# Four transformer layers on one core: three of six attentions made with the keys on partitions

## The chip, the cores and the metric

One core of one Trainium2 chip runs the kernel. The metric is the device time in microseconds (us) of one execution; less is better. The median of three runs of the kernel before is 3726.12 us (3721.3 to 3736.9).

## The reference

A batch of 64 elements of 128 tokens and 128 features (fp32), with a context of 77 tokens per element, goes through four layers:

- **L0**: self attention (16 heads, rope, causal), cross attention with the context (16 heads, rope, no mask), a gelu MLP of 512.
- **L1**: self attention (16 heads, no mask), cross attention (16 heads, no mask), then a mixture of experts: of 8 experts the two best per token.
- **L2**: a Mamba-2 block, then cross attention with 8 heads and one mask of keys.
- **L3**: cross attention with 16 heads and a mask of pairs, a last layer norm.

```python
s = jnp.einsum('blhd,bmhd->bhlm', q, k)        # 8 features per head; rope on q and k in L0
p = jax.nn.softmax(s, axis=-1)
a = jnp.einsum('bhlm,bmhd->blhd', p, v)
x = x + (a @ wo + bo)
```

## The kernel before

**Tiling.** The batch is cut into 16 passes of four elements (`NB` = 4), and the passes go round four streams, each with tiles of its own; four passes are a group. A pass is a first half (L0, L1 up to the routing) and a second half (the gathered experts' rows, L2, L3). A stream's order is first(g+1), second(g), and so on, so the last second half runs by itself. A fifth stream holds the experts: 20 pairs of blocks per group (`take` and `take_down` fetch rows and weights on the SP queue, then `block_turn`, `block_up`, `block_down`, `give`).

**The six attentions** are the list `ATT`: L0s and L0c in layer 0, L1s and L1c in layer 1, L2c, L3c. L0s and L1s have 128 keys, the others 77; all but L2c have 16 heads. Their steps, per element b:

- `spread` (GpSimd, line 2576): the element's keys times a 0/1 pattern, four heads beside each other, so that one product over 32 rows gives the scores of four heads.
- `scores` (TensorE, lines 1918 and 1923): where there is a mask, a bf16 product that writes it, then four fp32 products on 32 rows each (two on 64 rows for L2c), each into a bank of PSUM of its own. Queries stand on partitions, 4 x 77 or 4 x 128 scores in a bank.
- `soft` (VectorE, lines 2320 and 2326, then ScalarE, line 2155), by halves of eight heads: the maximum over the keys, the subtraction into SBUF, the exponential in place.
- `turn` (TensorE, line 1933, then ScalarE, line 2164), by quads of four heads: each head's probabilities are transposed, because the product with the values needs the keys on partitions, and copied out of PSUM.
- `mix` (TensorE, line 1945, ScalarE, line 2173), by halves: per head one product with the values, which carry a column of ones for the sum; four heads side by side in four column groups.
- `regroup` (TensorE, line 1953, VectorE, lines 2335 and 2336): four transposes back (two for L2c), and the division by the sum.

Ahead of them are norms (lines 2276 to 2279, 2544 to 2547, 2114, 1874, 2135), projections (line 1892; `rope` also multiplies by weights with swapped halves, line 1894, and combines both on VectorE, lines 2296 to 2299) and `values` (lines 1901 and 2307).

**What sets the order.** `timetable` simulates all five streams with a cost for each step (`parts`), the steps it waits for (`inputs_of`) and the free PSUM banks, and takes per engine the step with the least key: its time plus terms from tables (`LEAD`, `PHASES`, `STAY`, `EAGER`, `AHEAD`), which `CHANGES` replaces each 60 us of its plan. `STAY` is the price of a change of ScalarE's function table:

```python
key = (t + lead * (work[n][m] + PHASES[n]) - eager.get((step[0], engine), 0.0) - ahead.get(attention_of(step), 0.0)
       + (stay if switch else 0.0))
```

`Plan` sorts each engine's steps by the result. On the chip each engine runs that fixed list in order and waits on semaphores. The eight banks of PSUM are dealt out by the same plan: four to `scores`, two to `rope`, one to any other step with a product.

## Time and profile before

| | |
|---|---|
| median of three runs | 3726.12 us (3721.3 to 3736.9) |
| profiled execution | 3734.74 us, of which the span of instructions is 3732.9 us |
| mean granted TensorE clock | 0.952 |
| busy: TensorE / its weight loads | 3195.7 us (86%) / 2269.6 us (61%) |
| busy: VectorE / ScalarE / GpSimd | 2605.4 (70%) / 2652.3 (71%) / 1246.9 us (33%) |
| DMA | 212.98 MB, mean 57 GB/s |

PE is the matrix engine, PEld its weight loads (they overlap PE), DVE is VectorE, ACT ScalarE, POOL GpSimd, SP the queue that issues most DMAs. "L1933" is line 1933 of the kernel. A group's row gives what it writes and reads, shapes and count, then busy time and the mean of one; after the bar stand the idle time of the engine just ahead of the group and what ended it. Busy time is a union over the group, so overlapping matmuls are counted once, and busy divided by count is what one costs the engine. An fp32 matmul that isn't a transpose appears as two records.

### The profile page before, as it was taken

What the parts mean: (1) busy time and instruction counts of PE and PEld (TensorE: products, weight loads), DVE (VectorE), ACT (ScalarE), POOL (GpSimd) and SP (SyncE); (2) the same over time, 40 slices, a digit from 0 to 9 for tenths busy, and PEclk for the clock granted to TensorE, in tenths of its full rate; (3) what the DMA queues carried; (4) which work ended last, traced back from release to release, by engine and by line L of the source; (5) the groups of instructions that cost most, each with busy time, mean ns of one, the idle gap of its engine ahead of it and who ended that gap; (6) DMA issues with size and microseconds to landing.
All of it is one profiled execution on the core that took longest, in us unless ns stands there. A gap on an engine that the chain in (4) does not pass through costs nothing.

```text
span 3732.9 us, 87645 instructions
## 1 busy us (share of the span) xinstructions
PE 3195.7 (86%) x30064; PEld 2269.6 (61%) x30064; DVE 2605.4 (70%) x5408; ACT 2652.3 (71%) x5088; POOL 1246.9 (33%) x1615
## 2 busy tenths in 40 slices
PE   6898888888888979998988888998888997777897
PEld 3566556566756657665665656666565665665565
DVE  7877787755477777556888777665888877326775
ACT  4777777777876757887776766788776776656566
POOL 3122333212153353112244244212235434214632
PEclk9999999999999989999999999999999998989899
DMA  7013200134410033221000014322000004442000
GB/s 280 1 43 135 109 6 15 30 97 108 103 37 3 18 100 89 69 64 43 19 22 14 3 44 109 83 72 57 26 23 20 6 19 108 103 112 59 16 2 13
DMA packets 211920, 212.98 MB, mean 57 GB/s; under 512 B 51808, under 2 KB 155168, under 8 KB 211232
## 3 DMA queue, kind: packets, MB, share of 16 engines
q1 hardware_dynamic: 203296, 190.58, 18.1%
q0 software_dynamic: 8192, 16.79, 1.5%
q8 instruction: 252, 4.13, 0.5%
q14 instruction: 180, 1.47, 0.1%
HBM read 135.98 MB, written 71.30 MB: 56 GB/s over the span
## 4 chain that ended last, share of the span: by engine, by line
PE 39%; DVE 23%; ACT 15%; issue 8%; SPq 7%; DMA 4%; POOL 4%; ACTq 0%; DVEq 0%; POOLq 0%
PE ps L1933 8%; DVE mx L2320 6%; PE ps L1923 5%; PE ps L1945 4%; DVE pr L2326 4%; DMA b_up<-cols 4%; ACT block_hid L2211 3%; ACT pt L2164 3%; PE ps L1892 3%; PE ps L1953 2%; PE ps L2005 2%; PE ps L1918 2%; DVE kx L2326 2%; ACT xh L2114 2%; SPq L1818 1%
## 5 line engine op out<-in xcount | busy, mean ns | idle before, releaser
L2320 DVE TENSOR_REDUCE mx<-ps 128x8 f32<-128x616 f32 (+1 forms) x704 | 671.4, 954 | 334.7 <-PE ps L1923 316.4
L2164 ACT ACTIVATE pt<-ps 77x512 f32<-77x512 f32 (+1 forms) x1408 | 768.9, 593 | 126.1 <-PE ps L1933 123.2
L2576 POOL TENSOR_TENSOR kx<-kT,in_tiles 128x308 f32<-128x308 f32 (+1 forms) x384 | 315.7, 822 | 830.5 <-PE ps L1923 740.0
L1933 PE MATMUL ps<-k_sb,pr 128*77 128x128 f32 (+1 forms) x3776 | 538.9, 284 | 33.9 <-ACT pr L2155 10.3
L1933 PEld LDWEIGHTS ps<-k_sb,pr 128*77 128x77 f32 (+1 forms) x3776 | 421.1, 147 | 142.2 <-issue 73.2
L1945 PE MATMUL ps<-pt,v 77*16 77x128 f32 (+2 forms) x11264 | 444.3, 278 | 29.0 <-ACT pt L2164 11.2
L2326 DVE TENSOR_TENSOR pr<-ps,mx 128x616 f32<-128x616 f32 (+1 forms) x472 | 450.3, 954 | 16.2
L2155 ACT ACTIVATE pr<-pr 128x616 f32<-128x616 f32 (+1 forms) x472 | 392.7, 840 | 75.6 <-DVE pr L2326 74.6
L2173 ACT ACTIVATE og<-ps 128x256 f32<-128x256 f32 x704 | 267.3, 381 | 236.8 <-PE ps L1945 233.6
L1923 PE MATMUL ps<-kx,qT 32*128 32x308 f32 (+2 forms) x2816 | 361.6, 547 | 42.2 <-ACT pt L2164 15.8
L1945 PEld LDWEIGHTS ps<-pt,v 77*16 77x16 f32 (+2 forms) x11264 | 251.8, 97 | 181.1 <-issue 85.1
L2544 POOL TENSOR_SCALAR dt_p<-mv 128x4 f32<-128x4 f32 (+1 forms) x144 | 35.3, 245 | 942.8 <-DVE mv L2279 940.5
L1953 PE MATMUL ps<-k_sb,og 128*128 128x128 f32 x1408 | 232.8, 286 | 54.4 <-ACT og L2173 48.1
L1933 PE MATMUL ps<-k_sb,kx 128*77 128x128 f32 (+1 forms) x1856 | 267.2, 284 | 11.1 <-DVE pr L2326 4.7
L1953 PEld LDWEIGHTS ps<-k_sb,og 128*128 128x128 f32 x1408 | 154.7, 143 | 181.7 <-ACT og L2173 71.1
L2114 ACT ACTIVATE xh<-x,dt_p,rstd 128x128 f32<-128x128 f32 x448 | 184.3, 485 | 87.8 <-POOL dt_p L2547 85.9
L1933 PEld LDWEIGHTS ps<-k_sb,kx 128*77 128x77 f32 (+1 forms) x1856 | 208.2, 148 | 63.0 <-issue 33.7
L2326 DVE TENSOR_TENSOR kx<-ps,mx 128x616 f32<-128x616 f32 (+1 forms) x232 | 221.1, 953 | 8.0
L2155 ACT ACTIVATE kx<-kx 128x616 f32<-128x616 f32 (+1 forms) x232 | 194.3, 839 | 45.1 <-DVE kx L2326 44.3
L2335 DVE RECIPROCAL rc<-ps 128x16 f32<-128x16 f32 (+1 forms) x384 | 95.5, 249 | 184.8 <-PE ps L1953 174.1
L1923 PEld LDWEIGHTS ps<-kx,qT 32*128 32x128 f32 (+1 forms) x2816 | 125.1, 189 | 145.1 <-issue 104.9
L2005 PEld LDWEIGHTS ps<-block_cols,w_up 128*128 128x128 f32 x1280 | 183.0, 224 | 35.7 <-issue 14.9
(209 smaller groups left out, 5733.3 us busy)
## 6 DMA issues: line engine op xcount, KB each, us to landing
w_up<-weights SPq DMA_DIRECT2D x160, 256.0 KB
w_down<-weights SPq DMA_DIRECT2D x160, 256.0 KB
sent<-block_hid SPq DMA_DIRECT2D x42, 512.0 KB, 6.3
made<-block_hid SPq DMA_DIRECT2D x42, 512.0 KB, 6.3
block_rows<-sent SPq DMA_DIRECT2D x160, 64.0 KB
b_down<-expert_b SPq DMA_DIRECT2D x160, 64.0 KB
made<-block_out SPq DMA_DIRECT2D x160, 64.0 KB, 2.2
cT<-ctx_cols SPq DMA_DIRECT2D x32, 154.0 KB, 3.1
```

Of the source, the lines that this page charges most:

```text
L1923: i = mm(o, qT[s][r, b * L:(b + 1) * L], spread_keys[s][r, pl.slot(("spread", a, s, b), 2), 0:4 * keys], start=mask is None, stop=True)
L1933: i = tr(p[0:keys, j * L:(j + 1) * L], probs[s][pl.slot(unit, 3)][:, c:c + keys], ident)
L1945: i = mm(ps[32 * j:32 * j + t.slot, pl.banks[step][0], q * L:(q + 1) * L], heads_of(s, t)[0:keys, n, :], pt[s][0:keys, q, j * L:(j + 1) * ...
L1953: i = tr(p[:, q * L:(q + 1) * L], og[:, s % S, q * L:(q + 1) * L], ident)
L2005: i = mm(p[:, c * L:(c + 1) * L], w_up[:, j, c * 128:(c + 1) * 128], block_cols[:, j * L:(j + 1) * L], start=True, stop=True)
L2114: i = go_act(xh[s][0:m, b, :], src[0:m, b, :], ACT.Identity, scale=rstd[s][0:m, b:b + 1], bias=shift[s][0:m, b:b + 1])
L2155: go_act(v, v, ACT.Exp, scale=t.scale).then_inc(probs_ready.sem, 1)
L2164: go_act(pt[s][0:keys, q % 2, :], p[0:keys, :], ACT.Copy).then_inc(probsT_ready.sem, 1)
L2173: go_act(og[:, s % S, 2 * h * L:2 * (h + 1) * L], p[:, 0:2 * L], ACT.Copy)\
L2320: link(v_.tensor_reduce(m, tile, AX.X, ALU.max, negate=True))
L2326: tell(dve, v_.tensor_tensor(dst, tile, m.rearrange("p (c h) -> p c h", c=2).unsqueeze(3).broadcast_to([128, 2, 4, keys]), ALU.add), score ...
L2576: tell(pool, g_.tensor_tensor(spread_keys[s][:, pl.slot(step, 2), 0:4 * keys].rearrange("p (h k) -> p h k", h=4), kT[s][:, b * keys:(b + 1 ...
```

## The change

L0c, L1s and L1c get the mark `flip`; L0c and L1c (16 heads, 77 keys) are `flat` as well. For a marked attention `soft` and `turn` fall away. In their place:

- `scores` as before; `peak` (VectorE) takes only the negated maximum of each head.
- `split` (GpSimd) cuts it into three bf16 pieces, whose sum it is; `shift` turns the pieces on TensorE with one bf16 product, and VectorE copies them to SBUF as bf16.
- `scores_t` (TensorE) makes the scores again with operands exchanged, so that the keys are on partitions, and adds the maximum by a bf16 product with a 0/1 pattern. In L1s that is four chunks, one per head of a quad, of 128 keys; in the flat form the 4 x 77 = 308 rows of four heads are cut into three chunks of 128, 128 and 52. It takes four banks.
- `exp` (ScalarE), by halves, reads PSUM and writes the probabilities where `mix` reads them.
- In the flat form `mix` is 12 products of 32 columns of weights, since a chunk holds rows of up to three heads: the values must stand in chunks too, zero where a row is another head's. `blank` (ScalarE) writes zeros and ones, `chunk` (SP) copies the values into place with six DMAs from SBUF to SBUF, once per attention and pass. `regroup` turns three tiles, and VectorE adds the two parts of the heads that lie in two chunks.

Beside that, `rope` makes one product, not two: the swap of halves is a shuffle on VectorE (`SWAP`), so it takes one bank, and the swapped weights and biases aren't sent. The keys' buffer holds three elements for a marked attention, and `spread` of a following attention waits for the last `mix` of the one before; `gather` waits for a `mix` where it waited for a `turn`. The tables `expert_of` and `row_of` hold two groups in turn. Some costs in `parts` are other numbers, and all tables of the planner (`LEAD` to `CHANGES`) are replaced; `STAY` goes from 0.6307 to 312.6533. The core of the diff, its indentation cut:

```diff
+PIECES = 3
...
+self.flat = flip and heads == 16 and keys == LC
+self.spreads = 3 if flip else 2
+self.pitch = 4 * keys if self.flat else 4 * L
...
 Attention("L0c", 16, LC, "L0_ca_wq", "L0_ca_wk", "L0_ca_wv", "L0_ca_wo", "L0_ca_bq", "L0_ca_bk", "L0_ca_bv",
-          "L0_ca_bo", rope=True, norm=1),
+          "L0_ca_bo", rope=True, norm=1, flip=True),
 Attention("L1s", 16, L, "L1_sa_wq", "L1_sa_wk", "L1_sa_wv", "L1_sa_wo", "L1_sa_bq", "L1_sa_bk", "L1_sa_bv",
-          "L1_sa_bo", norm=3),
+          "L1_sa_bo", norm=3, flip=True),
 Attention("L1c", 16, LC, "L1_ca_wq", "L1_ca_wk", "L1_ca_wv", "L1_ca_wo", "L1_ca_bq", "L1_ca_bk", "L1_ca_bv",
-          "L1_ca_bo", norm=4, kv_norm=5),
+          "L1_ca_bo", norm=4, kv_norm=5, flip=True),
 Attention("L2c", 8, LC, "L2_wq", "L2_wk", "L2_wv", "L2_wo", mask="keys", norm=8),
...
+if t.flat:
+    values = [("blank", a, s)] + values + [("chunk", a, s)]
...
+def flipped_steps(a, s):
+    t = ATT[a]
+    out = [("spread", a, s, 0)]
+    turned = t.halves - 1 if t.flat else 0
+    for n in range(NB + 2):
+        if n < NB:
+            out.append(("scores", a, s, n))
+            if n + 1 < NB:
+                out.append(("spread", a, s, n + 1))
+            out += [("peak", a, s, n, h) for h in range(t.halves)]
+        if 1 <= n <= NB:
+            out.append(("shift", a, s, n - 1))
+        if n < NB:
+            out.append(("split", a, s, n))
+        if n >= 3:
+            out.append(("regroup", a, s, n - 3))
+        if n >= 2:
+            out.append(("mix", a, s, n - 2, turned))
+        if 1 <= n <= NB:
+            out.append(("scores_t", a, s, n - 1))
+            out += [("exp", a, s, n - 1, h) for h in range(t.halves)]
+        if n >= 2 and t.halves == 2 and not t.flat:
+            out.append(("mix", a, s, n - 2, 1))
+    return out
...
-last[b] = ("soft", *step[1:], n // 2) if step[0] == "scores" else step
+user = {"scores": "peak" if step[0] == "scores" and ATT[step[1]].flip else "soft", "scores_t": "exp"}.get(step[0])
+last[b] = (user, *step[1:], n // 2) if user else step
...
+def spread_keys(s, t, b):
+    at = b % t.spreads * t.pitch
+    return flat_kx[s][:, at:at + 4 * t.keys]
...
+def value_rows(s, c):
+    at = FLAT_V + 3 * ROW * c
+    return flat_kx[s][:, at:at + 32 * 16] if c < 2 else flat_pr[s][:, 12 * L:12 * L + 32 * 16]
...
+elif kind == "chunk":
+    a, s = step[1:]
+    sp.wait_ge(*blanked(a, s))
+    sp.wait_ge(*values_ready(a, s))
+    for c in range(3):
+        for slot, (j, key, row, n) in enumerate(pieces_of_chunk(c)):
+            sp.dma_start(value_rows(s, c)[row:row + n, slot * ROW:slot * ROW + 128],
+                         flat_v1[s][key:key + n, j * 128:(j + 1) * 128]).then_inc(chunks_in[s], 16)
...
 i = mm(p[:, 0:n], W(w), src[:, 0:n], start=True, stop=True)
-if t.rope:
-    i = mm(bank(pl, step, 1)[:, 0:n], W(w + "r"), src[:, 0:n], start=True, stop=True)
 i.then_inc((rope_made if t.rope else projected).sem, 1)
...
+elif kind == "shift":
+    a, s, b = args
+    pe.wait_ge(*peaks_split(a, s, b))
+    mm(p[:, 0:L], pieces[:, s % S, :], ident16, start=True, stop=True).then_inc(shift_turned.sem, 1)
+elif kind == "scores_t":
+    a, s, b = args
+    t, keys = of_attention(a)
+    pe.wait_ge(*shift_ready(a, s, b))
+    tiles = t.heads // 4
+    high = 128 // tiles
+    masked = t.mask in ("causal", "pairs")
+    if masked and t.flat:
+        for c in range(3):
+            lo, n = c * 128, min(128, 4 * keys - c * 128)
+            for g in range(tiles):
+                mm(bank(pl, step, g)[0:n, lo:lo + L], mp16[s][:, b, lo % keys:lo % keys + n], ident16, start=True, stop=False)
+    elif masked:
+        mask = causal16 if t.mask == "causal" else mp16[s][:, b, 0:LC]
+        for g in range(tiles):
+            mm(bank(pl, step, g)[0:keys, :].rearrange("p (h q) -> p h q", h=4), mask,
+               ident16.unsqueeze(1).broadcast_to([128, 4, L]), start=True, stop=False)
+    each = 128 if t.flat else keys
+    for lo in range(0, 4 * keys, each):
+        n, c = min(each, 4 * keys - lo), lo // each * L
+        for g in range(tiles):
+            r = slice(high * g, high * (g + 1))
+            mm(bank(pl, step, g)[0:n, c:c + L], spread_keys(s, t, b)[r, lo:lo + n], qT[s][r, b * L:(b + 1) * L],
+               start=not masked, stop=False)
+        for g in range(tiles):
+            r = slice(high * g, high * g + 32)
+            own = fours16[r, lo:lo + n] if t.keys == LC else in_fours16[r, lo // L:lo // L + 1].broadcast_to([32, L])
+            i = mm(bank(pl, step, g)[0:n, c:c + L], own, shifts(s, t)[r, :], start=False,
+                   stop=not masked or t.flat or lo + n == 4 * keys)
+    i.then_inc(scores_turned.sem, 1)
 elif kind == "mix":
...
+if t.flat:
+    pe.wait_ge(chunks_in[s], 6 * 16 * (pl.rank["chunk", a, s] + 1))
+    for half in range(2):
+        pe.wait_ge(*probs_ready(a, s, b, half))
+    mine = [probs_by_key(s, t, pl.slot(("exp", a, s, b, half), 3)) for half in range(2)]
+    for c in range(3):
+        n = min(128, 4 * keys - c * 128)
+        for g in range(4):
+            at = (g % 2 * 3 + c) * L
+            i = mm(ps[32 * g:32 * g + 32, pl.banks[step][0], c * L:(c + 1) * L],
+                   value_rows(s, c).rearrange("p (w n) -> p w n", n=16)[0:n, :, g * NB + b],
+                   mine[g // 2][0:n, at:at + L], start=True, stop=True)
+    i.then_inc(mixed.sem, 1)
+    continue
+if t.flip:
...
-for q in range(t.quads):
+for q in range(3 if t.flat else t.quads):
...
+elif kind == "exp":
+    a, s, b, h = args
+    t, keys = of_attention(a)
+    act.wait_ge(*scores_turned(a, s, b))
+    old = pl.earlier(step, 3)
+    if old:
+        act.wait_ge(*mixed(*old[1:4], 1 if ATT[old[1]].flat else old[4]))
+    lo = pl.banks["scores_t", a, s, b][2 * h]
+    wide, high = (3 * L, 128) if t.flat else (4 * L, keys)
+    dst = probs_by_key(s, t, pl.slot(step, 3))[0:high, :].rearrange("p (c x) -> p c x", c=2)
+    src = ps[0:high, lo:lo + 2, 0:wide]
+    if t.mask == "keys":
+        i = go_act(dst, src, ACT.Exp, scale=t.scale, bias=mk_col[0:keys, :])
+    else:
+        i = go_act(dst, src, ACT.Exp, scale=t.scale)
...
+if t.flat:
+    go_act(og[:, s % S, 0:3 * L], p[:, 0:3 * L], ACT.Copy).then_inc(gathered.sem, 1)
+    continue
...
+elif kind == "blank":
+    a, s = args
+    if s < S:
+        act.wait_ge(blanks_in, 6 * 16)
+    act.wait_ge(*mixed(a - 1, s, NB - 1, ATT[a - 1].halves - 1))
+    go_act(flat_kx[s][:, FLAT_V:FLAT_V + 59 * 16].rearrange("p (w n) -> p w n", n=16),
+           blanks[:, 0:59].unsqueeze(2).broadcast_to([128, 59, 16]), ACT.Copy)
+    go_act(value_rows(s, 2).rearrange("p (w n) -> p w n", n=16),
+           blanks[:, 59:91].unsqueeze(2).broadcast_to([128, 32, 16]), ACT.Copy).then_inc(blanked.sem, 1)
...
-link(v_.scalar_tensor_tensor(by_batch(dst[:]), by_batch(p), C(bias), table("cos"), ALU.add, ALU.mult))
-link(v_.scalar_tensor_tensor(by_batch(tmp[:]), by_batch(bank(pl, step, 1)), C(bias + "r"), table("sin"),
-                             ALU.add, ALU.mult))
-tell(dve, v_.tensor_tensor(dst[:, 0:NB * m], dst[:, 0:NB * m], tmp[:, 0:NB * m], ALU.add),
+link(v_.scalar_tensor_tensor(by_batch(tmp[:]), by_batch(p), C(bias), table("sin"), ALU.add, ALU.mult))
+v_.scalar_tensor_tensor(by_batch(dst[:]), by_batch(p), C(bias), table("cos"), ALU.add, ALU.mult)
+link(v_.stream_shuffle(tmp[:, 0:NB * m], tmp[:, 0:NB * m], SWAP))
+tell(dve, v_.tensor_tensor(dst[:, 0:NB * m], dst[:, 0:NB * m], tmp[:, 0:NB * m], ALU.subtract),
...
+elif kind == "peak":
+    a, s, b, h = args
+    t, keys = of_attention(a)
+    dve.wait_ge(*scores_made(a, s, b))
+    old = pl.earlier(("spread", a, s, b), 1)
+    if old and ATT[old[1]].flip:
+        dve.wait_ge(*peaks_split(*old[1:]))
+    lo = pl.banks["scores", a, s, b][2 * h]
+    tile = ps[:, lo:lo + 2, 0:4 * keys].rearrange("p c (h k) -> p c h k", h=4)
+    tell(dve, v_.tensor_reduce(peaks[:, s % S, 8 * h:8 * h + 8], tile, AX.X, ALU.max, negate=True),
+         peaks_found, *args)
+elif kind == "shift":
+    a, s, b = args
+    dve.wait_ge(*shift_turned(a, s, b))
+    old = pl.earlier(("spread", a, s, b), 1)
+    if old and ATT[old[1]].flip:
+        dve.wait_ge(*scores_turned(*old[1:]))
+    t, keys = of_attention(a)
+    tell(dve, v_.tensor_copy(shifts(s, t), p[:, 0:L]), shift_ready, a, s, b)
 elif kind == "regroup":
...
+def pair(at, n):
+    return p[:, at:at + 2 * n].rearrange("p (j x) -> p j x", j=2)[:, :, 0:128].rearrange("p j (g r) -> p j g r", g=4)
+whole, parted = pair(0, 137)[:, :, :, 0:9], split_heads[:].rearrange("p (j g w) -> p j g w", j=2, g=4)
+of_whole, of_parted = (rc[:, 8 * k:8 * k + 8].rearrange("p (j g) -> p j g", j=2) for k in range(2))
+result = xh[s][:, b, :].rearrange("p (g j two w) -> p two j g w", g=4, two=2, w=8)
+v_.reciprocal(of_whole, whole[:, :, :, 8])
+link(v_.tensor_copy(parted, pair(128, 128)[:, :, :, 0:9]))
+link(v_.tensor_tensor(parted, pair(9, 137)[:, :, :, 0:9], parted, ALU.add))
+link(v_.reciprocal(of_parted, parted[:, :, :, 8]))
+v_.tensor_tensor(result[:, 0], whole[:, :, :, 0:8], of_whole.unsqueeze(3).broadcast_to([128, 2, 4, 8]), ALU.mult)
+tell(dve, v_.tensor_tensor(result[:, 1], parted[:, :, :, 0:8], of_parted.unsqueeze(3).broadcast_to([128, 2, 4, 8]),
+                           ALU.mult), heads_ready, a, s, b)
+continue
...
-old = pl.earlier(step, 2)
-if old:
-    pool.wait_ge(*scores_made(*old[1:]))
+if b >= t.spreads or a not in (0, 4):
+    used = last_use(a, s, b)
...
+t, keys = of_attention(a)
+tiles = t.heads // 4
+rows_of = pieces[:, s % S, :].rearrange("p (g i j) -> p i g j", g=tiles, j=4)
+part = [rows_of[:, n, :, :] for n in range(PIECES)]
+peak, rest = (x[:, 0:t.heads].rearrange("p (g j) -> p g j", j=4) for x in (peaks[:, s % S, :], rests))
+pool.wait_ge(*peaks_found(a, s, b, t.halves - 1))
+old = pl.earlier(("spread", a, s, b), 1)
+if old and ATT[old[1]].flip:
+    pool.wait_ge(*shift_turned(*old[1:]))
+link(g_.tensor_copy(part[0], peak))
+link(g_.tensor_tensor(rest, peak, part[0], ALU.subtract))
+link(g_.tensor_copy(part[1], rest))
+tell(pool, g_.tensor_tensor(part[2], rest, part[1], ALU.subtract), peaks_split, a, s, b)
```

## Rows read from the trace of the kernel before

**Rows 1.** The page's busy line: busy us, share of the span, instructions

```profile
PE 3195.7 (86%) x30064; PEld 2269.6 (61%) x30064; DVE 2605.4 (70%) x5408; ACT 2652.3 (71%) x5088; POOL 1246.9 (33%) x1615
```

**Rows 2.** The page's chain that ended last, by engine

```profile
PE 39%; DVE 23%; ACT 15%; issue 8%; SPq 7%; DMA 4%; POOL 4%; ACTq 0%; DVEq 0%; POOLq 0%
```

**Rows 3.** Stretches: from:to, length, busy PE PEld DVE ACT POOL, clock, DMA

```profile
1493.00:1679.00 186.00, 172.60 (x1750) 126.03 (x1748) 110.99 (x193) 153.69 (x295) 31.27 (x44) 0.99 0.27 67
...
0.00:3172.00 3172.00, 2746.52 (x26231) 1934.88 (x26232) 2295.39 (x4677) 2317.36 (x4422) 1052.88 (x1387) 0.96 0.20 58
3172.00:3732.00 560.00, 449.18 (x3834) 334.76 (x3833) 310.02 (x731) 334.96 (x667) 194.00 (x228) 0.91 0.20 51
```

**Rows 4.** PE's waits: who waited for whom, us in total, times, longest

```profile
PE ps L1999 <- DMA b_up<-cols: 108.2, 55, 4.6
...
PE ps L1923 <- ACT pt L2164: 15.8, 31, 1.0
```

**Rows 5.** Groups of PE by shape: count, busy us, mean ns, idle before

```profile
L1933 PE MATMUL ps<-k_sb,pr 128*77 128x128 f32 x2400 | 343.4, 284 | 14.4 <-DVE pr L2326 4.5 <-DVE kx L2326 2.7 <-DVE v L2307 1.7
L1945 PE MATMUL ps<-pt,v 77*16 77x128 f32 x6144 | 243.7, 277 | 14.9 <-ACT pt L2164 7.0 <-DVE pr L2326 3.6 <-DVE kx L2326 1.8
L1953 PE MATMUL ps<-k_sb,og 128*128 128x128 f32 x1408 | 232.8, 286 | 54.4 <-ACT og L2173 48.1 <-ACT block_hid L2211 2.6 <-DVE kx L2468 1.2
L1933 PE MATMUL ps<-k_sb,pr 128*128 128x128 f32 x1376 | 196.1, 284 | 19.5 <-ACT pr L2155 9.0 <-DVE kx L2326 3.9 <-DVE pr L2326 3.5
...
L1894 PE MATMUL ps<-hT,w_sb 128*128 128x512 f32 x96 | 51.6, 621 | 0.0
...
L1945 PE MATMUL ps<-pt,v 77*32 77x128 f32 x1024 | 41.7, 280 | 1.2 <-ACT pt L2164 1.2
...
L1894 PE MATMUL ps<-cT,w_sb 128*128 128x308 f32 x32 | 10.9, 422 | 0.0
```

**Rows 6.** Order of time, 1506 to 1516 us: start, length, engine, line

```profile
1507.94 0.21 PEld L1918 LDWEIGHTS ps<-mk,k 128*128 128x128 bf16 x2
1508.05 0.43 PE L1918 MATMUL ps<-mk,k 128*128 128x308 bf16 x2
...
1513.37 0.31 PEld L1923 LDWEIGHTS ps<-kx,qT 32*128 32x128 f32 x8 [0.42 <-issue]
1513.37 1.14 PE L1923 MATMUL ps<-kx,qT 32*128 32x512 f32 x8
```

**Rows 7.** Groups of DVE by shape

```profile
L2326 DVE TENSOR_TENSOR pr<-ps,mx 128x616 f32<-128x616 f32 x300 | 239.7, 799 | 10.3
L2326 DVE TENSOR_TENSOR pr<-ps,mx 128x1024 f32<-128x1024 f32 x172 | 210.5, 1224 | 5.9
...
L2336 DVE TENSOR_TENSOR xh<-ps,rc 128x128 f32<-128x128 f32 x384 | 111.7, 291 | 13.5
...
L2299 DVE TENSOR_TENSOR qT<-qT,tmp 128x512 f32<-128x512 f32 x32 | 27.4, 856 | 1.1
```

**Rows 8.** Groups of ACT by shape

```profile
L2164 ACT ACTIVATE pt<-ps 77x512 f32<-77x512 f32 x896 | 488.8, 591 | 85.4 <-PE ps L1933 83.4
...
L2173 ACT ACTIVATE og<-ps 128x256 f32<-128x256 f32 x704 | 267.3, 381 | 236.8 <-PE ps L1945 233.6
...
L2155 ACT ACTIVATE pr<-pr 128x616 f32<-128x616 f32 x300 | 212.1, 715 | 41.9 <-DVE pr L2326 41.3
...
L2155 ACT ACTIVATE pr<-pr 128x1024 f32<-128x1024 f32 x172 | 181.5, 1057 | 33.7 <-DVE pr L2326 33.3
...
L2211 ACT ACT_TABLE_LOAD x81 | 103.9, 1283 | 1.4
```

**Rows 9.** Groups of POOL

```profile
L2576 POOL TENSOR_TENSOR kx<-kT,in_tiles 128x308 f32<-128x308 f32 (+1 forms) x384 | 315.7, 822 | 830.5 <-PE ps L1923 740.0 <-issue 63.3 <-DVE kT L2299 8.7
...
L2544 POOL TENSOR_SCALAR dt_p<-mv 128x4 f32<-128x4 f32 (+1 forms) x144 | 35.3, 245 | 942.8 <-DVE mv L2279 940.5
```

**Rows 10.** The same order of time: a DMA issue on the SP queue

```profile
1505.87 0.33 SPq L1817 DMA_DIRECT2D block_rows<-sent  x1
```

1592 lines of the change are left out of this document (777 added, 815 removed).

## The prediction

> **What bounds the kernel now.** The busy line first: PE 3195.7 us of a span of 3732.9, 86%, against 70% for DVE, 71% for ACT and 33% for POOL [rows 1]. Then the chain of waits: PE holds 39% of it, DVE 23%, ACT 15%, the SP queue 7% [rows 2]. So no engine is a wall by itself; PE is the fullest, and the others take their turns in the chain. The table by stretches places it: up to 3172 us PE is busy 2746.5 us (86.6%), in its best stretch, 1493 to 1679, 172.6 of 186 (92.8%), and in the last 560 us 449 (80%) [rows 3]. That last part matters: by the order of the steps a second half (attentions L2c and L3c, no part of the change) of one group runs last, with the experts of the last group before it, so what the change saves lies ahead of about 3172 us. PE's waits say that its idle time is spread: the longest single cause is the expert rows' DMA, 108.2 us, and a bank that another step's copy still holds is small, 15.8 us for the scores behind the copies of L2164 [rows 4]. I read from this that PE work is the currency, and that idle time goes with it as long as no new wait appears.
>
> **PE, what goes.** Line 1933 turns the probabilities: 16 transposes per batch element, 64 elements, per attention. One costs 343.4/2400 = 0.143 us of PE, with 128 keys 196.1/1376 = 0.143 too [rows 5], so 2.29 us per element and attention, in L0c, L1s and L1c. In L0c and L1c (the flat form) the 16 small products with the values become 12. The profile shows such a product as two records: 6144 records for three attentions of 1024 products, 243.7 us, 0.079 us each [rows 5]; that a product now has 32 columns of weights changes it little (2 x 41.7/1024 = 0.081 in L2c). So 1.27 becomes 0.97, 0.30 less. One of four regroup transposes goes, 232.8/1408 = 0.165 [rows 5]. And the rope of L0s and L0c no longer multiplies by the swapped weights: line 1894 goes whole, 51.6 + 10.9 = 62.5 us [rows 5].
>
> **PE, what comes.** "scores_t" makes the scores again with keys on partitions: per chunk of 128 rows four products of fp32 on 32 rows each with 128 moving columns, and four of bf16 that add the row maximum. Nothing in the trace has this shape; the nearest is the scores step, also four groups of 32 rows. Its eight weight loads took 0.31 us together, 0.039 each, and its eight matmul records with 512 moving columns 1.14 us; two whole bf16 loads took 0.21 [rows 6]. Moving columns are a quarter here, so weights set the pace: 0.31 for fp32 and four more at 0.039, 0.47 us per chunk if the streaming hides below them. That is 1.4 us for three chunks (flat), 1.9 for four (L1s). From above: streams that hide nothing add a quarter of what lies between, (1.14 - 0.31)/4 = 0.21 for fp32 and about 0.06 for bf16, so 0.74 per chunk, 2.2 and 3.0. From below: three times the mix rate of rows 5, 0.32 per four products, with bf16 free, 0.95 and 1.3. I take 0.47, since the loads are what those rows show most directly. The "shift" product is one bf16 matmul with 128 columns, about 0.1 (half of 0.21).
>
> The Trainium skill speaks against this value. "TensorE: Matmul & The Clock Gate", section "LDWEIGHTS", says a load's time goes by its columns at P/1.2 ns and that 32 rows cost as much as 128; by that estimate a chunk's twelve loads, taken singly, would need 1.28 us instead of 0.47. The trace disagrees for 32 rows: eight such loads were done in 0.31 [rows 6], where the rule gives 0.85. With the page's figure the sum for PE would turn positive; it stays as a rival.
>
> Sum for PE: flat, per element, -2.29 - 0.30 - 0.17 + 0.10 + 1.40 = -1.26, times 128 = -161 us. L1s: -2.29 + 0.10 + 1.90 = -0.29, times 64 = -19. Rope -62. Together -242 us of 3196.
>
> **The other engines.** They are not the currency but must not become it. DVE: the subtraction of L2326 goes (256 x 0.799 + 128 x 1.224 = -361 us), the maximum stays; a copy of the shift comes (192 x about 0.29, as L2336, the nearest of 128 columns = +56); the flat regroup has six small operations where there were two, about four more of 0.2 to 0.29 (+128 x 0.95 = +122); the rope gets a shuffle, which no row shows: from 0.291 to the 0.856 of the addition L2299, 48 times at 512 columns and 16 at 308; I take a little under the upper end, +45 [rows 7]. Net -138 of 2605. ACT: 768 copies of turned probabilities at 488.8/896 = 0.546 go, -419; evictions of the mix go from 256 of 0.381 to 128 of about 0.49, -35; the exponentials of the flat form widen from 616 to 768 columns, between 0.715 and 1.057, +0.13 x 256 = +33; "blank" writes zeros, 32 x 1.6 = +51 [rows 8]. Net -370 of 2652. POOL: "split" cuts the maximum into three bf16 pieces, 192 x 4 small operations of about 0.25 [rows 9], +190 to +230 with their links, to some 1460 us, 43%. SP: "chunk" issues six DMAs, 32 times; an issue takes 0.33 us [rows 10], so 2.0 us each, 64 us in all, queued ahead of the experts' "take". The data itself lands two elements before the first mix needs it, behind projections and norms; the SP time is hidden by the stretches without experts, and if each of the 24 chunks beside experts delayed a take by its 2.0, 48 us more would stand in the wait of rows 4. I take nothing and keep the 48 in the range. POOL's "spread" of a following attention now also waits for the last mix of the one before in its stream; behind it on POOL stand the other streams' spreads, sums and indirect DMAs. The planner knows that wait and orders POOL by it, and POOL is idle for two thirds of the span, so I price it at nothing; a late spread would add its own 0.82 us [rows 9] before 64 attentions, 53 us at most, in the range too.
>
> The tables of priorities are replaced whole, so all steps stand in another order. No row prices an order: zero, from the gain of the first rival to the loss of the banks. One entry can be read: the price of changing ACT's function table rises from 0.63 to 312, which keeps equal functions together; the largest group of table loads alone takes 103.9 us of ACT now [rows 8], more room on an engine that is not full.
>
> **From PE work to time.** The saving lies ahead of 3172 us. If idle time stays what it is, 3734.7 (the profiled execution) - 242 = 3493. If PE's share stays 86.6%, 242/0.866 = 280, so 3455. DVE and ACT, which hold 38% of the chain, also lose 5% and 14%, so I take the second. The three runs have their median at 3726.1, 8.6 us under the profiled execution; the forecast is 3726 - 280 = 3446, said as 3450. Its own range is 3400 to 3500.
>
> **Rivals.**
> - *The idle time shrinks too.* For: ACT loses 370 us, and ACT and DVE hold 38% of the chain [rows 2]. Against: the new steps add hops. If the share ahead of 3172 goes halfway to 92.8%, to 89.7%, it is (2746 - 242)/0.897 + 561 = 3353. 19%.
> - *The second scores hide no streaming* (0.74 per chunk). That gives back (0.8 x 128 + 1.1 x 64)/0.866 = 200, so 3650. 6%.
> - *Banks.* "scores_t" takes four of the eight banks as "scores" does, and must wait until an exponential frees a pair. For: both steps of one stream alone fill PSUM. Against: the waits for banks in rows 4 are small with four banks taken by one step and one by each other. At one exponential of 0.84 us for each of 192 steps: +161, 3611. The Trainium skill says the same under "TensorEngine Tiling (Array Packing)", "PSUM Pressure": row tiles go to different banks. 13%.
> - *Slower: PE waits for the shift.* Before, a turn waited for one DVE and one ACT operation. Now maximum, split on POOL (about 1.0 us and its links), shift on PE, copy on DVE (0.29) stand in a row before "scores_t", all in queues whose order is fixed. The order puts the next element's scores and maxima between, which covers it if POOL is on time; behind an indirect DMA or a bias addition it isn't. It decides from 280/192 = 1.46 us of wait per element on; at one whole split and copy, 1.6 us, it is 3450 + 307 = 3757. 6%.
> - *Slower: weight loads one after another.* A load of 128 columns at the turn's rate, under 0.143 us, 36 times per flat element and 48 in L1s: 5.1 and 6.9 instead of 1.4 and 1.9, some +790 us. Rows 6 speak against it. The page on TensorE named above states this rule. 1%.
> - *The gain is hidden* by the expert chain or a lower clock (0.91 in the last part against 0.96 before [rows 3]): about 3726. 3%.
>
> **How the numbers follow.** 52% for the forecast. Faster by over 0.5% (what a measurement of this kernel can tell from no change, its three runs lying within 0.4%) takes in the forecast, the shrinking idle time, the case that hides no streaming and the banks: 90%. Within 0.5%: 3%. Slower: 7%. The range goes down past 3353 to 3320, which leaves out about 6%, and up to 3640, which takes in the bank case, the 48 us of SP and part of the next; some 14% lie above.
>
> **What would show it.** Right: line 1933 with 1024 + 512 + 1024 transposes (L0s, L2c, L3c) and about 365 us instead of 5632 x 0.143 = 805; no second rope product; PE busy near 2950; "scores_t" groups near 1.4 and 1.9 us in the order of time; the last 560 us as now. Wrong: scores_t above 2.2; "scores_t" or "shift" high among PE's waits, with POOL or the DVE copy as releaser (the chain), or with ACT (the banks); PE's share under 83%. The forecast falls if PE busy drops as said and the span doesn't follow, or if PE busy doesn't drop.

## The result and the profile after

The changed kernel takes 3838.1 us (median of 4 runs, 3830.2 to 3839.3) against 3726.4 us for the kernel before: ratio 1.029, interval 1.027 to 1.032. The forecast was 3450 us. The sign was wrong.

The busy line of the changed kernel:

```profile
PE 3139.7 (82%) x33584; PEld 2199.1 (57%) x33584; DVE 2413.3 (63%) x5893; ACT 2293.0 (60%) x4236; POOL 1411.6 (37%) x2390
```

Against [rows 1], DVE lost 192 us (forecast 138), ACT 359 (370), POOL gained 165 (190 to 230). PE lost only 56 where 242 were forecast, and its idle time rose from 537 us (3732.9 - 3195.7) to 696 (3835.8 - 3139.7). Idle time that grows by 159 and work that shrinks by 56 make the 103 us by which the span grew. No engine became fuller except POOL, at 37%.

The granted clock, in the stretches of [rows 3] (same columns):

```profile
0.00:3172.00 3172.00, 2614.31 (x29351) 1806.60 (x29352) 2053.64 (x5054) 1908.90 (x3476) 1188.81 (x2132) 0.92 0.20 57
3172.00:3836.00 664.00, 525.37 (x4234) 392.52 (x4232) 359.66 (x839) 384.13 (x761) 222.78 (x259) 0.87 0.22 55
```

The clock is 0.92 and 0.87 where it was 0.96 and 0.91; over the whole span 0.912 against 0.952. The clock has two levels in the trace, 1.2 and 2.4 GHz, so 0.952 is some 358 us of the span at the lower one and 0.912 some 675. The share of PE up to 3172 us is 82.4%, not 86.6%.

Behind the last product of the router (line 1984, 2038 in the changed kernel) only steps are left whose instructions the change leaves as they are. That rest took 649 us before and takes 688 (first before, then after):

```profile
3084.00:3733.00 649.00, 517.95 (x4321) 386.41 (x4321) 374.15 (x904) 388.56 (x776) 236.52 (x276) 0.90 0.23 59
3148.00:3836.00 688.00, 543.30 (x4403) 406.13 (x4402) 378.96 (x915) 394.93 (x784) 240.04 (x281) 0.87 0.22 55
```

With 2% more records it takes 6% longer: 39 of the 103 us are lost where no new step stands, against the forecast's "the last 560 us as now".

PE's waits (columns as in [rows 4]):

```profile
PE ps L2053 <- DMA b_up<-cols: 138.5, 49, 7.0
PE ps L1874 <- ACT xh L2168: 46.3, 24, 19.7
PE ps L1892 <- ACT hT L2189: 39.1, 53, 2.1
PE ps L2019 <- ACT hT L2266: 27.9, 46, 1.2
PE ps L1961 <- DVE kx L2440: 20.6, 36, 1.9
...
PE ps L1961 <- ACT pt L2218: 12.0, 7, 3.9
```

The new chain, "scores_t" (L1961) behind the copy of the shift (L2440), costs 20.6 us in all, and the banks (behind L2218, the copy of turned probabilities) 12.0. The wait for the experts' rows (line 2053, 1999 before) grew by 30 us; the rest is spread, much of it over steps that the change doesn't touch, such as the projections behind ACT's copies (L1892, 39.1 us for 19.5) and the outputs (L2019, 27.9 for 9.0).

How much of PE each kind of step really took can't be read from the groups, since the records of two lines lie over each other. So I counted each matmul record from its start to the start of the next (or to its own end where PE then idled); these sum to the busy time of the page. In us, with the records in brackets:

```
                        before            after           difference
turns                   743.7 (5632)      347.2 (2560)     -396.5
mix                     407.7 (11264)     406.8 (10240)      -0.9
regroup                 193.7 (1408)      195.9 (1280)       +2.2
second rope product      54.0 (128)       -                 -54.0
scores_t                -                 273.0 (7680)     +273.0
shift                   -                  26.2 (192)       +26.2
all other steps        1796.6            1890.6             +94.0
sum                    3195.7            3139.7             -56.0
```

The steps of the change give -150 us, and the steps that it doesn't touch take 94 us more. They have the same instructions; 1890.6/1796.6 is 5.2%, and the clock fell by 4.2%, which by itself would make 79 of the 94 us.

"scores_t" itself in order of time, L1s, four chunks at the full clock (start, length, engine, line):

```profile
723.73 0.40 PE L1961 MATMUL ps<-qT,kx 32*128 32x128 f32 x8
723.95 0.23 PE L1966 MATMUL ps<-kx,in_fours 32*128 32x128 bf16 x4
724.01 0.46 PE L1961 MATMUL ps<-qT,kx 32*128 32x128 f32 x8
724.29 0.23 PE L1966 MATMUL ps<-kx,in_fours 32*128 32x128 bf16 x4
724.34 0.46 PE L1961 MATMUL ps<-qT,kx 32*128 32x128 f32 x8
724.62 0.23 PE L1966 MATMUL ps<-kx,in_fours 32*128 32x128 bf16 x4
724.67 0.46 PE L1961 MATMUL ps<-qT,kx 32*128 32x128 f32 x8
724.95 0.23 PE L1966 MATMUL ps<-kx,in_fours 32*128 32x128 bf16 x4
```

The chunks start 0.33 us apart (724.01, 724.34, 724.67). A whole step takes 1.49 us at the full clock in L1s and 1.25 in the flat form, so 0.37 and 0.42 for a chunk; the mean of all 640 chunks is 273.0/640 = 0.43. The price of 0.47 was too high, not too low.

### The profile page after: what moved, and what is told of

It is laid out like the page before. It is cut to its first block, busy times and chain, and to the rows that moved or that the text cites. A ratio compares the mean times of both kernels' runs of the same rounds, so it can differ in the third digit from the quotient of the medians.

```text
span 3835.8 us, 94634 instructions
## 1 busy us (share of the span) xinstructions
PE 3139.7 (82%) x33584; PEld 2199.1 (57%) x33584; DVE 2413.3 (63%) x5893; ACT 2293.0 (60%) x4236; POOL 1411.6 (37%) x2390
## 4 chain that ended last, share of the span: by engine, by line
PE 31%; DVE 12%; ACT 8%; issue 6%; SPq 5%; POOL 5%; DMA 2%; DVEq 0%; POOLq 0%; ACTq 0%
PE ps L1921 4%; PE ps L1931 3%; PE ps L2059 2%; PE ps L1961 2%; PE ps L1999 2%; DMA b_up<-cols 2%; PE ps L1892 2%; DVE mx L2412 2%; PE ps L2116 2%; DVE peaks L2430 2%; PE ps L1916 2%; PE ps L2007 1%; ACT block_hid L2294 1%; PE ps L2019 1%; DVE pr L2418 1%
## 5 line engine op out<-in xcount | busy, mean ns | idle before, releaser
L2412 DVE TENSOR_REDUCE mx<-ps 128x8 f32<-128x616 f32 (+1 forms) x320 | 310.1, 969 | 328.2 <-PE ps L1921 321.4
L2430 DVE TENSOR_REDUCE peaks<-ps 128x8 f32<-128x616 f32 (+1 forms) x384 | 361.3, 941 | 190.7 <-PE ps L1921 135.4
L2218 ACT ACTIVATE pt<-ps 77x512 f32<-77x512 f32 (+1 forms) x640 | 352.6, 594 | 77.1 <-PE ps L1931 75.8
L1961 PE MATMUL ps<-qT,kx 32*128 32x128 f32 (+1 forms) x5120 | 272.5, 315 | 59.9 <-DVE kx L2440 20.6
L2233 ACT ACTIVATE pr<-ps 128x768 f32<-128x768 f32 (+1 forms) x256 | 217.2, 874 | 137.9 <-PE ps L1966 137.5
L1961 PEld LDWEIGHTS ps<-qT,kx 32*128 32x128 f32 (+1 forms) x5120 | 200.7, 181 | 130.4 <-issue 73.7
L1931 PE MATMUL ps<-k_sb,pr 128*77 128x128 f32 (+1 forms) x1728 | 254.5, 287 | 11.8 <-DVE pr L2418 2.8
L1999 PE MATMUL ps<-pt,v 128*16 128x128 f32 (+2 forms) x5888 | 240.8, 284 | 14.5 <-ACT pt L2218 7.9
L1931 PEld LDWEIGHTS ps<-k_sb,pr 128*77 128x77 f32 (+1 forms) x1728 | 197.7, 150 | 65.1 <-issue 32.7
L2059 PE MATMUL ps<-block_cols,w_up 128*128 128x128 f32 x1280 | 212.4, 334 | 14.9 <-ACT block_cols L2285 14.7
L2418 DVE TENSOR_TENSOR pr<-ps,mx 128x616 f32<-128x616 f32 (+1 forms) x216 | 210.0, 972 | 7.4
```

Source lines behind the costliest of these rows:

```text
L1931: i = tr(p[0:keys, j * L:(j + 1) * L], probs[s][pl.slot(unit, 3)][:, c:c + keys], ident)
L1961: mm(bank(pl, step, g)[0:n, c:c + L], spread_keys(s, t, b)[r, lo:lo + n], qT[s][r, b * L:(b + 1) * L], start=not masked, stop=False)
L1999: i = mm(ps[32 * j:32 * j + t.slot, pl.banks[step][0], q * L:(q + 1) * L], heads_of(s, t)[0:keys, n, :], mine[0:keys, (4 * q + j) * L:(4 * ...
L2059: i = mm(p[:, c * L:(c + 1) * L], w_up[:, j, c * 128:(c + 1) * 128], block_cols[:, j * L:(j + 1) * L], start=True, stop=True)
L2218: go_act(pt[s][0:keys, q % 2, :], p[0:keys, :], ACT.Copy).then_inc(probsT_ready.sem, 1)
L2233: i = go_act(dst, src, ACT.Exp, scale=t.scale)
```

## The experiments

Two batches (the four kernels of experiments 1 to 3, and the pair after_retuned_b and before_retuned_b) ran where the kernel before itself took 3892 us in place of 3727. Each ratio is against the kernel before of the same batch; ratios of those two batches are compared only among themselves.

**1. Is it the order of the steps?** The changed kernel with `flip=True` taken off the three attentions, once with the new tables of priorities and once with those of before. What is left of the change is the rope.

> The same with the new tables, so that only the order differs from the run above. Order theory: 3800 us or more even without one flipped attention. Cost theory: within 1.5% of the run above, 3650 to 3750.

> The changed kernel with no attention flipped and with the priority tables of the kernel before: the rope's swap on VectorE is nearly all that is left of the change. Cost theory (the flipped steps are dear on PE): 3660 to 3700 us, since the second rope products (62.5 us of PE) go. Order theory (the loss is in the new tables): the same, so this run is the base for the next one. If the rope's shuffle on VectorE is what hurts: 3740 or more.

Measured: 1.116 (1.113 to 1.120) and 1.122 (1.119 to 1.126). PE's share falls to 78% and 77%. A kernel that has less for TensorE to do than the kernel before (29936 records for 30064) is 12% slower, with either set of tables; no expectation had such a size. That it is the order is shown by rope_only_retuned in experiment 8: the same instructions (but for the loads of function tables) under mended costs and another order, and 0.980 in another batch, where one and the same kernel moves by 1% between two such batches (0.963 and 0.973, experiment 8). So an order can be worth several times what the change is, and my step that prices it at zero had no ground. These two say nothing of the change itself, though.

**2. The weights of the flat mix.** Line 1984 reads its weights with a stride; here it reads 32 columns that lie together (a constant, so the output is another).

```diff
-  value_rows(s, c).rearrange("p (w n) -> p w n", n=16)[0:n, :, g * NB + b],
+  K("upto")[0:n, 96:128],
```

> The changed kernel, same order, but the 12 products of the flat mix take 32 adjacent columns of a constant as weights in place of the values 16 columns apart (the attention's result is left wrong, the waits stay). Cost theory, stride part: the flat mix falls from 1.88 to about 1.0 us per element, 128 x 0.88 = 110 us of PE, and the span to about 3730. If the width or the 128 rows cost it and not the stride: mix stays at 1.8, time within 0.5% of 3838. Order or chain theory: PE busy falls but the time by less than half of it.

**3. The chain of the shift.** The bf16 products (L1966) and the wait for the shift are left out; the exponential's scale is cut by a thousand, so that values stay finite. The shift is still made.

```diff
-                    pe.wait_ge(*shift_ready(a, s, b))
...
-                            i = mm(bank(pl, step, g)[0:n, c:c + L], own, shifts(s, t)[r, :], start=False,
-                                   stop=not masked or t.flat or lo + n == 4 * keys)
```

> The changed kernel, same order, with the bf16 products of the row maximum left out of the second scores and with them the wait for the shift (the exponential takes a smaller factor so that it stays finite); maximum, split, shift and its copy still run. Chain theory: idle time of PE falls by 100 us or more and the time by more than the 162 us of those products. Cost theory: the time falls by 100 to 160 us, with idle time about as it is.

Measured, 2: 1.020 (1.017 to 1.023). Line 1984 is as dear as before (3072 records in 140.7 us, counted from start to start, for 136.2 at the higher clock of the changed kernel), so the stride costs nothing. Nothing else is changed in it, so it can stand for the changed kernel in this batch.

Measured, 3: 1.009 (1.006 to 1.013), 1.1% under 2. The busy lines of 2 and 3, whose spans are 3971.9 and 3926.9 us:

```profile
PE 3191.4 (80%) x33584; PEld 2215.8 (56%) x33584; DVE 2415.3 (61%) x5893; ACT 2292.3 (58%) x4236; POOL 1408.9 (35%) x2390
```

```profile
PE 3138.0 (80%) x31024; PEld 2171.2 (55%) x31024; DVE 2414.7 (61%) x5893; ACT 2291.9 (58%) x4236; POOL 1409.3 (36%) x2390
```

PE has 53 us less to do, and it idles for 781 us in 2 and 789 in 3, where the chain theory asked for 100 us less. Without the wait for the shift and with 2560 products fewer the kernel is still slower than before. The chain isn't the cause of the reversal.

**4. TensorE's work alone.** The kernel before in its own order, with one transpose in place of four in each turn step of the three attentions. The copy after it reads that quarter four times, so that ACT's work stays.

```diff
-                    for j in range(4):
+                    for j in range(1 if a in (1, 2, 3) else 4):
...
+                    turned = p[0:keys, 0:L].unsqueeze(1).broadcast_to([keys, 4, L])
```

> The kernel before, its order and every other engine's work untouched, but 1 transpose in place of 4 in each of the 768 turn steps of the attentions L0c, L1s and L1c (the copy after it reads the first quarter four times): 2304 transposes at the 0.132 us of a record fewer, 304 us of TensorE. The forecast's rule (TensorE's share is kept, work divided by 0.866) gives -351 us, a ratio near 0.906. If TensorE's work counts one for one, -304 us, 0.918. If the order and the other engines hold the steps where they are, so that removed TensorE time turns into idle time and a lower granted clock, less than a third of it comes back: 0.97 to 1.00, with the mean clock below 0.93.

> The changed kernel as it stands, once more on the chip of these runs, as the yardstick for the other kernels of this batch. If the time depends on the chip in the same way for both kernels, the ratio to the kernel before is again 1.029, within 0.005. If the loss were an accident of one chip's clock, it would be within 0.01 of 1.

Measured: few_turns 1.0145 (1.012 to 1.017), and the changed kernel again 1.028 (1.026 to 1.030). So the kernel before gets **slower** by 1.5% when 2304 of its transposes are taken away and nothing else but the source of the copy is touched. The expectations went from 0.906 to 1.00; the clock below 0.93 came as said, the time is beyond all of them. Its clock, busy line and a stretch of it:

```profile
core 0: 3780.9 us, clock 0.911
```

```profile
PE 3118.2 (82%) x27760; PEld 2101.9 (56%) x27760; DVE 2607.3 (69%) x5408; ACT 2645.6 (70%) x5088; POOL 1248.9 (33%) x1615
```

```profile
384.00:768.00 384.00, 314.77 (x2810) 187.58 (x2807) 288.39 (x574) 263.29 (x496) 124.96 (x173) 0.87 0.11 39
...
2688.00:3072.00 384.00, 316.31 (x2860) 199.60 (x2857) 304.40 (x631) 273.76 (x517) 148.75 (x196) 0.90 0.06 17
```

In the kernel before these two stretches are

```profile
384.00:768.00 384.00, 328.75 (x3249) 220.03 (x3247) 295.50 (x572) 277.56 (x519) 132.48 (x182) 0.97 0.13 43
...
2688.00:3072.00 384.00, 336.12 (x3311) 231.56 (x3299) 307.07 (x660) 278.67 (x528) 152.59 (x200) 0.97 0.06 17
```

PE carries some 440 records fewer in each, and the clock granted is 0.87 and 0.90, not 0.97. Over the span PE's work falls by 78 us only: counted as above, the turns lose 197 (a lone transpose with nothing behind it shows its whole 0.27 us, so less goes than the 304 expected) and the others gain 120 at the lower clock. Idle time grows from 537 to 663. This is the changed kernel's picture in small: 0.952 to 0.911, share 86% to 82%, with none of its new steps. I read it so: the 197 us that went out turned into idle time, and the 120 that the others take longer at the lower clock lengthened the span in part. That is argued from these sums; no run keeps the clock up while the work goes.

**5. The transfers on SP.** One of six for each chunk step (`range(3)` to `range(1)`, and the first piece only; the flat mixes then read old values).

> The changed kernel with 1 of the 6 transfers of each of the 32 chunk steps on SP (values for the flat mixes left stale, all other work kept). In the trace a chunk step holds SP for 4.9 us, so about 130 us of SP's queue goes, ahead of the experts' loads that wait in the same queue. If those passes cause the longer wait for b_up (138.5 us against 108.2), that wait falls back to about 108 us and the ratio to the kernel before by 0.01 or more against the changed kernel of this batch. If the transfers are hidden, as forecast, less than 0.004.

Measured: 1.0246 (1.023 to 1.026) against 1.0281 (1.026 to 1.030) of the same batch; the wait for b_up is 134.8 us, against 139.1. The two intervals touch at their ends: 0.35% at best. A chunk step is dear (4.9 us of SP, forecast 2.0), but hidden, as forecast.

**6. Is the clock what was lost?** Idle transposes ahead of a step's wait, into the bank that the step is about to write, as many as the wait in the trace had room for.

```diff
                 p = bank(pl, step)
+                for _ in range(FILL.get(at_step, 0)):
+                    tr(p[:, 0:L], ident, ident)
```

> The changed kernel, same order, with 4084 idle transposes (of the identity, into the bank that the step is about to write, ahead of its wait for data) put into 486 steps that were idle for 0.3 us or more in its trace; 4084 x 0.109 us = 445 us of TensorE work that computes nothing. If the granted clock falls because TensorE waits, and the lower clock is what the change lost (0.912 after, 0.952 before), the clock rises to 0.95 or more and the time falls below the changed kernel's, to 1.01 or less against the kernel before. If the waits themselves are the loss and the clock is a bystander, nothing is gained: 1.028. If TensorE's amount of work sets the time, as the forecast had it, it rises by as much as doesn't fit the waits, 1.05 or more.

> The same with the kernel before: 3059 idle transposes, 333 us, in 396 steps. If the clock is the lever, this one gains less than the changed kernel does, since its clock is at 0.952 already: 0.97 to 0.99. If not, 1.00 to 1.03.

Measured: 1.037 (1.034 to 1.041) with the clock at 0.982, and 1.018 (1.015 to 1.020) at 0.984. The clock does what was expected, the time doesn't. The busy line of after_filled and the group of the idle transposes:

```profile
PE 3388.0 (88%) x37668; PEld 2485.6 (65%) x37668; DVE 2419.4 (63%) x5893; ACT 2287.2 (59%) x4236; POOL 1409.7 (37%) x2390
```

```profile
L1906 PE MATMUL ps<-k_sb 128*128 128x128 f32 x4084 | 567.5, 285 | 240.7 <-ACT hT L2232 30.7 <-DVE kx L2483 22.3 <-ACT hT L2309 19.0
```

Counted from start to start, the idle transposes take 508 us, so the kernel's own work is 3388 - 508 = 2880 where it was 3140, 260 us less; the ratio of the clocks, 0.912/0.982, makes 224 of them. Idle time fell by 233 (696 to 463). That isn't the 508 that went in: PE sat idle for 240.7 us ahead of these transposes themselves, since their step has to wait for its bank first. I take it that they then ran into the time when the data was there. What the clock gave, they took. So the clock can be bought back, but not for less than it costs, put in like this.

**7. An order for the true costs.** The planner works out the order from a table of costs. Held against the traces, most entries agree within some per cent, and a few don't. The order of time for SP in the changed kernel, from the end of an expert's gelu (ACT, L2294) at 825.86 us:

```profile
827.21 0.35 SPq L1817 DMA_DIRECT2D block_rows<-sent  x1
827.76 0.35 SPq L1818 DMA_DIRECT2D w_up<-weights  x1
828.31 0.33 SPq L1819 DMA_DIRECT2D b_up<-cols  x1
829.96 0.33 SPq L1817 DMA_DIRECT2D block_rows<-sent  x1
830.49 0.33 SPq L1818 DMA_DIRECT2D w_up<-weights  x1
831.01 0.33 SPq L1819 DMA_DIRECT2D b_up<-cols  x1
831.45 4.06 SPq L1772 DMA_DIRECT2D kx<-v  x5
```

and for PE:

```profile
829.31 1.14 PE L1921 MATMUL ps<-kx,qT 32*128 32x512 f32 x8
833.57 0.66 PE L2053 MATMUL ps<-k_sb,block_rows 128*128 128x128 f32 x2 [3.12 <-DMA b_up<-cols]
```

A "take" needs 5.2 us from the gelu to its last issue (between the issues SP loads and checks addresses), and the data is there 2.6 us later. The planner books 1.2 and 4.0. Both kernels have this error, and both stand waiting at this place, for 108.2 and 138.5 us. The changed one has errors of its own as well: its flat mix takes 0.98 us at the full clock (booked 0.8), scores_t 1.25 and 1.49 (1.1 and 1.3), chunk 4.9 of SP (0.6). The entries for `take_down`, `give` and the landing of both takes are mended as well.

```diff
-        return [(Y, 1.2)]
+        return [(Y, 5.6)]
...
-        return [(Y, 0.6)]
+        return [(Y, 4.9)]
...
-        return [(P, 1.1 + (0.7 if t.mask else 0.0) if t.flat else 1.3 + mask)]
+        return [(P, 1.245 + (0.7 if t.mask else 0.0) if t.flat else 1.487 + mask)]
...
-        key = (t + lead * (work[n][m] + PHASES[n]) - eager.get((step[0], engine), 0.0) - ahead.get(attention_of(step), 0.0)
-               + (stay if switch else 0.0))
+        key = t + WEIGHT * (DUE[n][ENGINES.index(engine)][at[n][engine]] / 1000)
```

DUE holds one due time for each step and engine: at first those of the kernel's own old order, then changed by a random search as long as the planned end fell. The instructions are the same but for a few more loads of function tables on ACT (4266 instructions for 4236, and 5093 for 5088); their order isn't.

> The changed kernel with its steps in another order and nothing else changed. The planner's costs are set to what the traces show: a take holds SP for 5.6 us (booked 1.2) and lands 2.4 later (4.0), take_down 3.4 (0.5), give 2.3 (0.3), chunk 4.9 (0.6), scores_t 1.25 and 1.49 (1.1 and 1.3), the flat mix 0.98 (0.8), mlp 3.65 (3.52); the tables of priorities are replaced by one due time for each step and engine, found by a search with these costs. Theory: the change was slower because its order was made for steps shorter than they are, so TensorE waits and its clock falls. Then this order brings it under the kernel before (0.94 to 0.98) with TensorE's share above 86% or its clock above 0.94. Rival: the second scores, the longer chain and the lower clock are the change's own and no order mends them: 1.00 to 1.03.

> The kernel before with the same corrected costs (those of its own steps) and due times found by the same search for the same time. It tells what the order gives without the change. Theory: about as much as for any kernel with a mis-booked take, 0.96 to 0.99, and less than the changed kernel gets, so that the change is worth 1 to 4% once both are ordered for their true costs. Rival: the change is worth nothing even then, and both ratios agree within 0.005 or this one is lower.

Measured: 0.981 (0.978 to 0.984) for the changed kernel, 0.974 (0.972 to 0.976) for the kernel before. Both beat the old one; the changed kernel gained 4.7% from its new order, the kernel before 2.6%. The changed one stays short of what the theory asked for (PE's share above 86% or a clock above 0.94; it has 84% and 0.931), and the rival came, that the kernel before is no slower than it. Costs, rule and order were changed together: no run has a new search with the old costs, so how much of either gain is due to the mended costs isn't shown.

**8. What of the change is left?** The rope alone; idle transposes in the longest waits only; and, for the error of such a statement, a second order for each kernel.

> The changed kernel with flip taken off all three attentions, so that of the change only the rope with one product and the permuted values stays; corrected costs and due times from a search of the same kind and time. TensorE loses 54 us of work against the kernel before and no step gets a longer chain. If the three turned attentions cause what is left of the loss (0.981 against 0.974), this one is at or below 0.974. If removed TensorE work as such is worth nothing, it is 0.974 within 0.004; if it is worth its price, 0.96. If the rope is the part that costs, above 0.98.

> after_retuned with 935 idle transposes (about 102 us) in 58 steps that waited for data for a microsecond or more in its trace, each count kept under the wait. If the clock is what is left of the loss, it rises from 0.931 to 0.95 or more and the time falls by 0.5 to 1.5%, to 0.966 to 0.976. If the transposes delay as much as the clock gives, as in after_filled, 0.981 or above.

> before_retuned with 436 idle transposes (about 48 us) in 36 such steps. Less to gain, since its clock is 0.961: 0.968 to 0.974 if the clock counts, 0.974 or above if not.

> The changed kernel with corrected costs and a second set of due times, from another start of the same search, which counts it as good as the first. If the order that is found matters little among good ones, it is 0.981 within 0.003, and the 0.6% to before_retuned belongs to the change. If orders that are reckoned equal differ on the chip by half a per cent or more, that difference is open.

> The kernel before with a second set of due times, reckoned 0.6% longer than the first. 0.974 to 0.982 if the reckoning carries over to the chip; below 0.974 or above 0.985 if it doesn't.

> after_retuned_b once more, beside before_retuned_2. If its 0.963 carries over, it is 0.963 to 0.970 and faster than before_retuned: then the change is worth something with a good order. If the order matters little, 0.978 to 0.984, as after_retuned had.

> before_retuned once more: 0.974 within 0.003 where the kernel before takes 3727 us; as in the first runs.

```
                        ratio   interval          clock  PE busy
rope_only_retuned       0.980   0.978 to 0.982    0.945  3139.5
after_retuned_filled    0.979   0.977 to 0.982    0.944  3137.6
before_retuned_filled   0.971   0.969 to 0.974    0.967  3193.8
after_retuned_b2        0.973   0.971 to 0.975    0.931  3053.6
before_retuned_2        0.973   0.972 to 0.975    0.956  3169.6
(the kernel before at 3892 us:)
after_retuned_b         0.963   0.962 to 0.965    0.911
before_retuned_b        0.982   0.980 to 0.984    0.932
```

after_retuned_b and after_retuned_b2 are one and the same kernel, and so are before_retuned and before_retuned_2. Two orders of the changed kernel that the search counts as equal stand at 0.981 and 0.973. That 0.8% is the error of all these comparisons, and within it rope_only, the changed kernel and the kernel before are one, where the kernel before takes 3727 us. rope_only at 0.980 fits none of its expectations clearly. Where the kernel before takes 3892 us the changed kernel leads its counterpart, 0.963 to 0.982; but before_retuned_b was reckoned 0.6% longer than before_retuned, and the 0.963 didn't carry over: beside before_retuned_2 the same kernel stands at 0.973, outside the 0.963 to 0.970 expected. The sharpest pair ran side by side, after_retuned_b2 and before_retuned_2. Their busy lines, in this order:

```profile
PE 3053.6 (84%) x33584; PEld 2128.9 (59%) x33584; DVE 2437.8 (67%) x5893; ACT 2316.6 (64%) x4262; POOL 1408.2 (39%) x2390
```

```profile
PE 3169.6 (87%) x30064; PEld 2254.0 (62%) x30064; DVE 2609.5 (72%) x5408; ACT 2639.8 (73%) x5093; POOL 1246.1 (34%) x1615
```

Their spans are 3629.6 and 3632.4 us. The changed kernel has 116 us less of PE, 172 less of DVE and 323 less of ACT, and its PE idles for 113 us more (576.0 against 462.8). Part of where the new order gained is one line of each kernel's waits, for after_retuned_b2

```profile
PE ps L2259 <- DMA b_up<-cols: 26.3, 30, 2.9
```

and for before_retuned_2

```profile
PE ps L2046 <- DMA b_up<-cols: 42.8, 29, 5.6
```

where 138.5 and 108.2 us stood before. before_retuned_filled is the fastest of all, 3623.7 us, 0.2% under its unfilled order, which the intervals don't tell apart; after_retuned_filled gained a clock of 0.944 for 0.931 and no time.

## Why the prediction was wrong

The step that failed is **from PE work to time**, "If PE's share stays 86.6%, 242/0.866 = 280", and with it the sentence of the first part that "PE work is the currency, and that idle time goes with it as long as no new wait appears". The new waits are small (20.6 us for the shift, 12.0 for the banks), and idle time still grew by 159 us; PE's share came out at 82%. few_turns (experiment 4) shows the step false by itself: 78 us less PE busy in the same order, the other engines' work as it was (ACT 2645.6 us for 2652.3), and 126 us more idle time, and a span 48 us longer (3780.9 for 3732.9). The order of the steps on every engine is fixed and the chain goes by turns through PE, DVE and ACT [rows 2]; that a step which ends earlier there mostly waits for the next one is how I read it.

**The clock.** The rival "the gain is hidden by the expert chain or a lower clock" came nearest, with 3%, and its 3726 us was a wrong end: the clock fell with PE's own work, and at 0.912 for 0.952 unchanged steps took 94 us more. The rows for this were there: 0.99 in the fullest stretch, 0.91 in the emptiest [rows 3]. I read them as a property of the stretches and not as something that my own change would move. The Trainium skill, "TensorE: Matmul & The Clock Gate", section "HAM oscillation — how this bites in real kernels", says that bursts of matmuls parted by waits are throttled again and again. The traces agree: 66 stretches at the lower level before, 104 in few_turns, 105 in the changed kernel.

**The order priced at zero.** The instructions of rope_only stand at 1.116 in one order (experiment 1) and at 0.980 in another (8), and experiment 7 shows that both kernels stood in orders made for costs that are off. The changed kernel had more such costs (its three new steps), and a new order gave it 4.7% against 2.6%; with new orders the two are equal. So that it was slower by 2.8% hangs on its order: what these runs leave to the change itself is nothing within some 0.8%, where the kernel before takes 3727 us. That the wrong costs are why its old order was the worse one is likely, and not shown. Why the kernel with less work on three engines isn't the faster one under a good order, whether through the clock alone or through the longer chain, stays open. Neither idle transposes nor leaving out the shift's wait settled it.

**The sizes, term by term.**

- Turns: 2.29 per element forecast; the table's 396.5 us over 192 elements are 2.07. The busy time of a group counts the end of each record that lies over the next, so 0.143 was too high (743.7/5632 = 0.132).
- Flat mix: 0.30 less forecast, about 0.1 found (32 records at 0.036 make 1.16, the 24 new ones 136.2/128 = 1.06); the rate per record was taken as fixed, and it rose to 0.044. The 32 columns aren't the reason: with them L2c's mix takes 37.3/1024 = 0.036 a record before, like those of 16 columns, and experiment 2 rules out the stride. In the flat mix the records of the two full chunks take 82.2/2048 = 0.040, where the clock alone makes 0.038 of 0.036, and those of the short third chunk, which end the step, 54.0/1024 = 0.053. Why is open.
- Regroup: -0.17 forecast, and 2.2 us more found in all; at the old rate the 1280 records would be 176 us, the lower clock makes 184 of it, and the last 12 fit a step with fewer transposes, which leaves more of the last one's 0.27 us in view.
- Shift: 0.10 and 0.14.
- Rope: -62 and -54.
- scores_t: 301 us forecast (1.4 and 1.9), 273 found even at the lower clock.

Together -150 where -242 was forecast; 92 us are mis-sized terms, and the other steps' 94, most of it the clock's, were no term at all. By the forecast's own rule even -56 would have been a gain; that it wasn't is the step above.

**Right:** the serial weight loads and the streams that hide nothing, both named as unlikely, did not come. By the figure of the Trainium skill ("TensorE: Matmul & The Clock Gate", section "LDWEIGHTS") a chunk's twelve loads are estimated at 1.28 us, taken singly. Here a chunk goes by in 0.33 to 0.43. The chain of the shift, my slower rival, is there and small. Of the other engines DVE's shuffle was priced "a little under the upper end" of 0.291 to 0.856; it takes 0.727. ACT's flat exponential lies between its bounds, at 0.808. SP's issues cost 0.7 to 0.9 each instead of 0.33, hidden all the same.

## What to carry to other kernels

An engine that is 86% busy in a kernel whose queues have a fixed order is not yet the bound: ask, before a removal is divided by the share, which wait would end earlier, and test it by taking the work out without changing the order. Expect the granted clock to fall with the idle time, and the steps that stay to take longer for it. Where a planner writes the order, hold its costs against a trace before judging a change by one run: mending the costs and the order was worth 2.6% to the old kernel, where the change under test was worth nothing that could be told, and new steps priced from a guess carry the error into everything that stands around them.
